# An adaLN condition and a feed-forward layer on one core: how q is projected, and who scales the first batch

## Chip, cores and metric

One core of one Trainium2 chip runs the whole kernel. The metric is the device time of one execution in microseconds, a median over runs. The engines are named TensorE (PE), its weight loads (PEld), VectorE (DVE), ScalarE (ACT), GpSimd (POOL) and SyncE (SP), as in the profile.

## Reference, cut to what matters

`x` is 16 x 512 x 1024, `cond` 16 x 512, all fp32.

```
q_emb = relu(cond @ W3 + b3)                     # 16 x 1024
u     = (512 * x + sum_over_512_rows(x)) * q_emb[:, None, :]
v     = relu(u @ W2 + b2)
ffn   = v @ W_base + b_base + (v @ A_s) @ B_s + routed low-rank experts(v)
out   = x + ffn
```

Everything waits for `q_emb`: no row of `u` exists without it. It is a small product (16 x 512 by 512 x 1024) in full fp32.

## The kernel before, in words

Data lie transposed: features on the 128 partitions, the 512 tokens of a batch in the free dimension. D = 1024 makes K = 8 tiles, or two halves of H = 4. Batches go in NP = 8 pairs (a, b); one pair is `g`, and for each pair the product with W2 is made as NPROD = 7 half-size products n = 0..6 (a Strassen scheme), later the same again with W_base. A product has H operand tiles k and H output tiles j. Each fp32 product is three matmuls in fp32r (function `three`): high x high, low x high, high x low; so both operands are split into a rounded high part (`act_hi`, `w_hi`) and a rest (`act_lo`, `w_lo`). TensorE runs 12 matmuls for each k of the first three products (`first_groups`), in the order k outer, j inner; each k waits for `lo_done` and `w2_lo_done`.

The order on every engine is written out by hand, one block per engine; each engine works its instructions off in order. DMAs are issued by SyncE and, six at the start, by ScalarE. Each 256 KB tile of W3 (`w3_raw`, half h, row block k), of W2 (`r11`, `r12`, ...) and of x (`src`) is one DMA.

The head of the kernel, which the change touches, before:

- TensorE warms up on `zeros` (`warm`), then `project(0, ...)` makes q's first half with the condition (128 x 16) as the held operand and W3's rows (128 x 512) streamed, so q lands as 16 rows by 512 in one bank. A copy to `qrow`, four transposes (`turn`) and q is feature-major, 128 x (4 x 16), in `q_tok`.
- VectorE's `condition(h)` adds b3 and makes relu(q) twice: `qn` (times T = 512) and `q1`.
- For x of batch a (quadrant G11) ScalarE sums each raw tile while q is not there (`first_total`), VectorE scales it by `qn` (`first_scale`) and multiplies the sum by `q1` to get the shift; ScalarE rounds the high part (`first_hi`), VectorE makes the low part (`low`). ScalarE also rounds W2's first tiles (`first_w2`), VectorE makes their low part (`first_w2_low`).
- The second half of W3 is projected before product 0 (`project(1, ...)`), copied by ScalarE, and transposed by `turn(1)` behind product 0's first k.
- `x_scale` is the one-instruction form used for the other quadrants: ScalarE scales a tile by `qn` and sums it in the same instruction.

ScalarE's function table is loaded by an ACT_TABLE_LOAD that the build puts right ahead of ScalarE's first ACTIVATE, behind any wait that stands alone in front of it.

Of the kernel before, what the change touches and what calls it, by code (L numbers as in the profile page):

```python
# [5 lines left out]
F32 = mybir.dt.float32  # L6
# [31 lines left out]
def adaln_ffn(nc, xT, condT, w3, w2, b2, wbase, bbase, acat, bcat, brouter, outT, E, R):  # L38
# [18 lines left out]
    with ExitStack() as ctx:  # L57
# [28 lines left out]
        qrow = sb("qrow", [NB, D], F32, early)  # L86
# [34 lines left out]
        q1 = sb("q1", [P, K, NB], F32, stage1)  # L121
# [4 lines left out]
        ident = sb("ident", [P, P], F32, stage1)  # L126
        sb("pad8", [P, T - K - 2 * K * NB - 9 * H - P], F32, stage1)
# [37 lines left out]
        Q_BANK, QT_BANK, WARM_BANK = 4, 6, 0  # L165
        q_tok = [ps[:, QT_BANK + h, 0:HALF * NB].rearrange("p (m b) -> p m b", b=NB) for h in range(2)]
# [9 lines left out]
        q_copied = sem("q_copied")  # L176
        q_turned = sem("q_turned")
# [18 lines left out]
        first_sum = sem("first_sum")  # L196
        first_mean = sem("first_mean")
        first_x1 = sem("first_x1")
# [84 lines left out]
        def scaled_no(i, q, k):  # L283

            return H * (i - (q == G11)) + k + 1
# [23 lines left out]
        def _(sp):  # L309
# [68 lines left out]
            load_w3(0, 2)  # L378
            load_w3(1, 0)
            load_x(0, G11, 0)  # L380
            load_w3(1, 2)
            for k in range(1, H):
                load_x(0, G11, k)
                load_w2(Q11, r11, k)
            for k in range(H):
                load_x(0, G21, k)
                load_w2(Q12, r12, k)
# [194 lines left out]
        def _(pool):  # L582

            nc.gpsimd.memset(ident[:], 0.0).then_inc(const_step, 1)
# [4 lines left out]
            pool.wait_ge(const_step, 2)  # L589
            nc.gpsimd.affine_select(out=ident[:], in_=ident[:], compare_op=ALU.not_equal, fill=1.0, base=0,  # L590
                                    pattern=[[-1, P]], channel_multiplier=1).then_inc(const_step, 1)
# [3 lines left out]
            def shift_of(i, q, ks=range(H)):  # L595

                for k in ks:
                    if q == G12:
                        pool.wait_ge(t1_made, four(i, k))
                    else:  # L600
                        pool.wait_ge(x_scaled[q], scaled_no(i, q, k))
# [34 lines left out]
        def _(act):  # L636
            def x_scale(i, q, k):
# [3 lines left out]
                if i == 0:  # L641
                    act.wait_ge(q_ready, 1 + HALF_OF[q])
                nc.scalar.activation(src[:, t, :], src[:, t, :], ACT.Identity,  # L643
# [106 lines left out]
            def first_hi(k):  # L750
                act.wait_ge(first_x1, k + 1)
# [4 lines left out]
            def first_w2(k):  # L756
                act.wait_ge(w2_loaded[H * Q11 + k], 16)
                nc.scalar.activation(w_hi[:, 0, k, :], r11[:, k, :], ACT.Copy).then_inc(first_hi_done, 1)

            def first_total(k):  # L760

                t = tile(G11, k)
                act.wait_ge(x_loaded[t], 16)
                nc.scalar.activation(act_lo[:, slot(0, 1, k), :], src[:, t, :], ACT.Copy,
                                     accum_out=vsum[:, t:t + 1]).then_inc(first_sum, 1)
# [3 lines left out]
            act.dma_start(w3_raw[:, 0, 3], w3[0, 3]).then_inc(w3_loaded[3], 16)  # L769
            act.dma_start(w3_raw[:, 1, 1], w3[1, 1]).then_inc(w3_loaded[QK + 1], 16)  # L770
            act.dma_start(r11[:, 0, :], w2[0, 0]).then_inc(w2_loaded[H * Q11], 16)
            act.dma_start(w3_raw[:, 1, 3], w3[1, 3]).then_inc(w3_loaded[QK + 3], 16)

            first_total(0)
            first_w2(0)
            first_hi(0)
            first_total(1)
            first_w2(1)
            act.wait_ge(q_sum, 2)
            nc.scalar.activation(qrow[:, D // 2:D], ps[0:NB, Q_BANK + 1, :], ACT.Copy).then_inc(q_copied, 1)  # L780
            first_total(2)
            first_hi(1)
            first_w2(2)
# [1054 lines left out]
```

## Time and profile before

| | |
|---|---|
| median of 3 runs | 1411.69 us (1411.1 to 1412.03) |
| the profiled execution | 1411.89 us, its span 1410.1 us |
| TensorE busy | 1405.7 us (100%), 6175 matmuls |
| VectorE, ScalarE, GpSimd busy | 910.6, 605.5, 22.1 us |
| PEclk | 9 (of 9) in all 40 slices |

The span runs from the first to the last instruction; 1.8 us of the execution lie outside it. Busy shares are of the span. The chain that ended last is followed back from the last instruction. PEclk is the clock that the throttle granted; it says nothing of a lower level in the first microseconds, which shows in the spacing of matmuls of one size.

### The profile page before, as it was taken

Reading aid. Unit: us, or ns where it says so; the run is one execution under the profiler, and the core shown is the slowest. Engines: PE = TensorE matmul, PEld = TensorE weight load, DVE = VectorE, ACT = ScalarE, POOL = GpSimd, SP = SyncE. Lnnn points to the kernel's source line nnn. Section 1 sums busy time; section 2 is a strip of 40 time slices with the busy share of each in tenths; the row PEclk is TensorE's granted clock in tenths of the full one; section 3 lists DMA queues with packets and bytes.
Section 4 is the critical chain, followed back from the end, with each engine's and each line's share of the span. In section 5 each row is a group of like instructions: output and inputs, shape, how many; then the busy total and the mean of one; then the engine's idle time right before and its main releaser. Section 6 shows DMA issues by size and latency. Waiting matters only on the chain.

```text
span 1410.1 us, 18033 instructions
## 1 busy us (share of the span) xinstructions
PE 1405.7 (100%) x6175; PEld 1155.8 (82%) x6175; DVE 910.6 (65%) x1563; ACT 605.5 (43%) x1136; POOL 22.1 (2%) x69
## 2 busy tenths in 40 slices
PE   9999999999999999999999999999999999999999
PEld 5888888888888888888888888888888888888887
DVE  6987565765656656567889665655655656556564
ACT  6774645546455464645544231332312323132230
POOL 3000000000000000000000000000000000000000
PEclk9999999999999999999999999999999999999999
DMA  8252414334142342426726527163361724617242
GB/s 314 67 173 82 155 54 139 106 90 155 52 141 98 104 148 59 142 83 224 266 89 208 195 95 249 61 222 136 109 239 63 246 105 136 216 60 258 94 148 91
DMA packets 135580, 200.03 MB, mean 142 GB/s; under 512 B 38752, under 2 KB 39008, under 8 KB 135488
## 3 DMA queue, kind: packets, MB, share of 16 engines
q1 hardware_dynamic: 134480, 197.39, 42.4%
q10 hardware_dynamic: 1008, 1.48, 0.3%
q8 instruction: 49, 0.80, 0.2%
q14 instruction: 43, 0.35, 0.1%
HBM read 127.12 MB, written 71.70 MB: 141 GB/s over the span
## 4 chain that ended last, share of the span: by engine, by line
PE 99%; DMA 0%; DVE 0%; DVEq 0%; issue 0%
PE ps L1611 33%; PE ps L1613 33%; PE ps L1612 33%; PE ps L1619 1%; DMA cond_b<-in_condT 0%; PE ps L1628 0%; DVE buf L1604 0%; DVEq L57 0%; PE ps L1634 0%
## 5 line engine op out<-in xcount | busy, mean ns | idle before, releaser
L1611 PE MATMUL ps<-act_hi,w_hi 128*128 128x512 f32 x1792 | 697.4, 389 | 0.0
L1612 PE MATMUL ps<-act_lo,w_hi 128*128 128x512 f32 x1792 | 697.1, 389 | 0.0
L1613 PE MATMUL ps<-act_hi,w_lo 128*128 128x512 f32 x1792 | 697.1, 389 | 0.0
L1611 PEld LDWEIGHTS ps<-act_hi,w_hi 128*128 128x128 f32 x1792 | 336.3, 188 | 70.1 <-DVE act_lo L1078 0.3
L1613 PEld LDWEIGHTS ps<-act_hi,w_lo 128*128 128x128 f32 x1792 | 336.3, 188 | 70.0
L1612 PEld LDWEIGHTS ps<-act_lo,w_hi 128*128 128x128 f32 x1792 | 336.3, 188 | 69.8
L681 ACT ACTIVATE act_hi<-src 128x512 fp32r<-128x512 f32 x256 | 156.4, 625 | 256.1 <-PE ps L1613 254.3
L1142 DVE SCALAR_TENSOR_TENSOR buf<-ps,bb_sb,buf 128x512 f32<-128x512 f32 x127 | 95.0, 749 | 157.3 <-PE ps L1613 142.3
L1085 DVE TENSOR_TENSOR act_lo<-src,act_hi 128x512 fp32r<-128x512 f32 x192 | 130.4, 684 | 36.5 <-ACT act_hi L681 36.5
L1078 DVE SCALAR_TENSOR_TENSOR act_lo<-src,shift,act_hi 128x512 fp32r<-128x512 f32 x128 | 95.2, 748 | 31.2 <-ACT act_hi L678 30.6
L700 ACT ACTIVATE yhi<-buf 128x512 fp32r<-128x512 f32 x128 | 80.0, 625 | 64.2 <-PE ps L1613 64.1
L1142 DVE SCALAR_TENSOR_TENSOR buf<-ps,b_sb,buf 128x512 f32<-128x512 f32 x92 | 68.8, 750 | 51.2 <-PE ps L1613 50.5
L1085 DVE TENSOR_TENSOR act_lo<-buf,act_hi 128x512 fp32r<-128x512 f32 x64 | 43.4, 687 | 84.6 <-ACT act_hi L681 84.5
L678 ACT ACTIVATE act_hi<-src,shift 128x512 fp32r<-128x512 f32 x124 | 87.5, 714 | 14.1 <-POOL shift L603 13.8
L708 ACT ACTIVATE buf<-ps 128x512 f32<-128x512 f32 x64 | 37.9, 597 | 120.5 <-PE ps L1613 120.5
L716 ACT ACTIVATE buf<-ps 128x512 f32<-128x512 f32 x64 | 37.9, 597 | 118.4 <-PE ps L1613 118.4
L1182 DVE TENSOR_TENSOR buf_lo<-buf,yhi 128x512 fp32r<-128x512 f32 x64 | 44.1, 688 | 55.5 <-ACT yhi L700 54.7
L727 ACT ACTIVATE buf<-ps 128x512 f32<-128x512 f32 x60 | 35.9, 598 | 84.1 <-PE ps L1613 84.1
L643 ACT ACTIVATE src<-src,qn 128x512 f32<-128x512 f32 x92 | 65.5, 712 | 0.9 <-DVE q L1047 0.9
L1082 DVE SCALAR_TENSOR_TENSOR act_lo<-src,act_hi 128x512 fp32r<-128x512 f32 x64 | 44.0, 688 | 33.2 <-ACT act_hi L681 33.1
L1611 PE MATMUL ps<-yhi,a_hi 128*128 128x512 f32 x128 | 49.8, 389 | 0.0
L1612 PE MATMUL ps<-buf_lo,a_hi 128*128 128x512 f32 x128 | 49.8, 389 | 0.0
(114 smaller groups left out, 1020.6 us busy)
## 6 DMA issues: line engine op xcount, KB each, us to landing
src<-in_xT SPq DMA_DIRECT2D x224, 256.0 KB, 2.9
y_scratch<-buf SPq DMA_DIRECT2D x128, 256.0 KB, 2.1
src<-y_scratch SPq DMA_DIRECT2D x128, 256.0 KB, 5.0
outT<-buf SPq DMA_DIRECT2D x127, 256.0 KB, 3.9
buf<-in_xT SPq DMA_DIRECT2D x32, 256.0 KB, 4.8
wl_raw<-in_wbase SPq DMA_DIRECT2D x6, 1024.0 KB, 5.9
r<-in_w SPq DMA_DIRECT2D x15, 256.0 KB, 9.6
grow<-gates_scratch SPq DMA_DIRECT2D x96, 32.0 KB, 2.1
```

Source lines behind the costliest of these rows:

```text
L643: nc.scalar.activation(src[:, t, :], src[:, t, :], ACT.Identity, scale=qn[:, H * HALF_OF[q] + k, 2 * i + BATCH_OF[q]:2 * i + BATCH_OF[q] + 1],
L678: nc.scalar.activation(act_hi[:, slot(g, n, k), :], source[:, t, :], ACT.Identity, bias=shift[:, t:t + 1]).then_inc(hi_done, 1)
L681: nc.scalar.activation(act_hi[:, slot(g, n, k), :], source[:, t, :], func).then_inc(hi_done, 1)
L700: nc.scalar.activation(yhi[:, (y_no(i, c, j) - 1) % 2, :], buf[:, j, :], func).then_inc(yhi_done, 1)
L1078: nc.vector.scalar_tensor_tensor(act_lo[:, s, :], source, shift[:, t:t + 1], act_hi[:, s, :].bitcast(F32), ALU.add, ALU.subtract).then_inc ...
L1082: nc.vector.scalar_tensor_tensor(act_lo[:, s, :], source, 0.0, act_hi[:, s, :].bitcast(F32), ALU.max, ALU.subtract).then_inc(lo_done, 1)
L1085: nc.vector.tensor_tensor(act_lo[:, s, :], source, act_hi[:, s, :].bitcast(F32), ALU.subtract).then_inc(lo_done, 1)
L1142: nc.vector.scalar_tensor_tensor(buf, ps[:, bank, :], bias, buf, ALU.add, ALU.add).then_inc(done, 1)
L1182: nc.vector.tensor_tensor(lo, y, hi, ALU.subtract).then_inc(ylo_done, 1)
L1611: nc.tensor.matmul(out, wh, a_h, start=start, stop=False, skip_group_check=onto)
L1612: nc.tensor.matmul(out, wh, a_l, start=False, stop=False, skip_group_check=onto)
L1613: return nc.tensor.matmul(out, wl, a_h, start=False, stop=stop, skip_group_check=onto)
```

## The change

It does these things:

1. `project` swaps the operands: each 128 x 128 block of W3 is held, the condition (128 x 16) is streamed. q comes out feature-major, with no copy and no transpose: 4 matmuls for each k, 32 in all in place of 8 matmuls and 8 transposes. `qrow`, `q1`, `ident`, `turn` go.
2. Batch a's first tiles are scaled and summed by ScalarE's `x_scale`, which waits for q; VectorE only multiplies the sum by 1/T (`first_shift`). `first_total` and `first_scale` go.
3. Of W3's second half, k = 0 is projected before product 0, k = 1 behind its first k, k = 2 and 3 behind its second. `condition(1)` stands behind product 0's last `low`.
4. 7 warm-up matmuls ahead and 6 between the halves, for 6 and 1.
5. The first tiles of x and W2 are loaded in two halves of 64 partitions, one by each queue; W3's second half is loaded later. ScalarE has seven DMA issues in front where it had six.

```diff
+            sp.dma_start(src[0:P // 2, tile(G11, 0), :], xT[0, 0, 0:P // 2]).then_inc(x_loaded[tile(G11, 0)], 16)
+            sp.dma_start(r11[0:P // 2, 0, :], w2[0, 0, 0:P // 2]).then_inc(w2_loaded[H * Q11], 16)
             load_w3(1, 0)
-            load_x(0, G11, 0)
+            load_w2(Q11, r11, 1)
+            load_x(0, G11, 2)
             load_w3(1, 2)
+            load_w3(1, 3)
...
                 if i == 0:
                     act.wait_ge(q_ready, 1 + HALF_OF[q])
+                    if t == tile(G11, 0):
+                        act.wait_ge(first_x_rest, 16)
...
+            act.dma_start(src[P // 2:P, tile(G11, 0), :], xT[0, 0, P // 2:P]).then_inc(first_x_rest, 16)
+            act.dma_start(r11[P // 2:P, 0, :], w2[0, 0, P // 2:P]).then_inc(first_w2_rest, 16)
+            act.dma_start(src[:, tile(G11, 1), :], xT[0, 1]).then_inc(x_loaded[tile(G11, 1)], 16)
             act.dma_start(w3_raw[:, 1, 1], w3[1, 1]).then_inc(w3_loaded[QK + 1], 16)
...
+            for k in range(H):
+                x_scale(0, G11, k)
+                first_w2(k)
+                first_hi(k)
             x_scale(0, G21, 0)
-            first_hi(3)
...
-                dve.wait_ge(q_turned, h + 1)
-                nc.vector.tensor_tensor(part, q_tok[h], bias, ALU.add).then_inc(q_biased, 1)
+                dve.wait_ge(q_sum, h + 1)
+                nc.vector.tensor_tensor(part, q_banks[h], bias, ALU.add).then_inc(q_biased, 1)
+                dve.wait_ge(q_biased, h + 1)
+                nc.vector.tensor_scalar(part, part, 0.0, float(T), ALU.max, ALU.mult).then_inc(q_ready, 1)
...
+            def first_shift(k):
                 t = tile(G11, k)
+                dve.wait_ge(x_scaled[G11], scaled_no(0, k))
+                nc.vector.tensor_scalar(shift[:, t:t + 1], vsum[:, t:t + 1], 1.0 / T, None,
                                         ALU.mult).then_inc(first_mean, 1)
+            for k in range(H):
+                first_shift(k)
                 first_w2_low(k)
                 low(0, 0, k)
+            condition(1)
...
-                    mm = nc.tensor.matmul(ps[0:NB, Q_BANK + h, :], cond_sb[:, k, :], w3_raw[:, h, k, :],
-                                          start=(k == 0), stop=(k == QK - 1))
+                    for m in range(HALF):
+                        mm = nc.tensor.matmul(ps[:, h * HALF + m, 0:NB],
+                                              w3_raw[:, h, k, m * P:(m + 1) * P], cond_sb[:, k, :],
+                                              start=(k == 0), stop=(k == QK - 1))
...
             pe.wait_ge(warm_set, 1)
-            warm(6)
+            warm(7)
             pe.wait_ge(cond_loaded, 16)
             project(0, range(QK))
+            warm(6)
             project(1, (0,))
-            pe.wait_ge(const_step, 3)
-            turn(0)
-            project(1, range(1, QK))
-            warm(1)
...
-                    if k == 0 and n == 0:
-                        turn(1)
+                    if n == 0 and k < 2:
+                        project(1, ((1,), (2, 3))[k])
```

**TensorE, from the first instruction to product 0.** A row is one matmul of the program, or xN equal ones; an fp32 one is executed as two weight loads and two passes. L1634 warms, L1619 projects, L1628 transposes, L1611 to L1613 are product 0. Before:

```order
L1634 MATMUL ps<-zeros 128x512 x6
L1619 MATMUL ps<-w_raw,cond_b 16x512 x5
L1628 MATMUL ps<-ident,qrow 128x16 x4
L1619 MATMUL ps<-w_raw,cond_b 16x512 x3
L1634 MATMUL ps<-zeros 128x512
L1611 MATMUL ps<-act_hi,w_hi 128x512
L1612 MATMUL ps<-act_lo,w_hi 128x512
L1613 MATMUL ps<-act_hi,w_lo 128x512
```

With the change (L1600 warms, L1592 projects, L1582 to L1584 are product 0):

```order
L1600 MATMUL ps<-zeros 128x512 x7
L1592 MATMUL ps<-cond_b,w_raw 128x16 x16
L1600 MATMUL ps<-zeros 128x512 x6
L1592 MATMUL ps<-cond_b,w_raw 128x16 x4
L1582 MATMUL ps<-act_hi,w_hi 128x512
L1583 MATMUL ps<-act_lo,w_hi 128x512
L1584 MATMUL ps<-act_hi,w_lo 128x512
```

The first projection is 16 small matmuls in place of 4 long ones, the transposes are gone, six warm-ups stand behind it, and one quarter of the second half's projection is left ahead of product 0.

**TensorE, behind the twelve matmuls of a k of product 0.** Before, behind k = 0:

```order
L1612 MATMUL ps<-act_lo,w_hi 128x512
L1613 MATMUL ps<-act_hi,w_lo 128x512
L1628 MATMUL ps<-ident,qrow 128x16 x4
L1611 MATMUL ps<-act_hi,w_hi 128x512
L1612 MATMUL ps<-act_lo,w_hi 128x512
```

With the change, behind k = 1 (behind k = 0 stand four):

```order
L1583 MATMUL ps<-act_lo,w_hi 128x512
L1584 MATMUL ps<-act_hi,w_lo 128x512
L1592 MATMUL ps<-cond_b,w_raw 128x16 x8
L1582 MATMUL ps<-act_hi,w_hi 128x512
L1583 MATMUL ps<-act_lo,w_hi 128x512
```

Eight projecting matmuls stand between the second and the third k, and four between the first and the second, where four transposes stood behind the first.

**ScalarE, from its last DMA issues to the second tile** (with the semaphores that each row, or a wait that stands alone ahead of it, waits for). Before:

```order
L772 DMA w_raw<-in_w 128x512
L764 ACT_TABLE_LOAD
L764 ACTIVATE act_lo,vsum<-src 128x512 [waits x_loaded0]
L758 ACTIVATE w_hi<-r 128x512 [waits w2_loaded0]
L753 ACTIVATE act_hi<-src,shift 128x512 [waits first_mean,first_x1]
L764 ACTIVATE act_lo,vsum<-src 128x512 [waits x_loaded1]
L758 ACTIVATE w_hi<-r 128x512 [waits w2_loaded1]
L780 ACTIVATE qrow<-ps 16x512 [waits q_sum]
L764 ACTIVATE act_lo,vsum<-src 128x512 [waits x_loaded2]
```

With the change (L644 is `x_scale`):

```order
L766 DMA r<-in_w 64x512
L767 DMA src<-in_xT 128x512
L768 DMA w_raw<-in_w 128x512
L644 ACT_TABLE_LOAD [waits first_x_rest,q_ready]
L644 ACTIVATE src,vsum<-src,qn 128x512 [waits x_loaded0]
L760 ACTIVATE w_hi<-r 128x512 [waits first_w2_rest,w2_loaded0]
L753 ACTIVATE act_hi<-src,shift 128x512 [waits first_mean]
L644 ACTIVATE src,vsum<-src,qn 128x512 [waits q_ready,x_loaded1]
L760 ACTIVATE w_hi<-r 128x512 [waits w2_loaded1]
```

The table load stands behind the waits for q (`q_ready`) and for the second half of x's first tile, where it stood behind no wait; the sum of the raw tile is gone, and the first thing that ScalarE computes needs q.

## Rows read from the trace of the kernel before

**Rows 1.** The page: chain that ended last, by line.
```profile
PE ps L1611 33%; PE ps L1613 33%; PE ps L1612 33%; PE ps L1619 1%; DMA cond_b<-in_condT 0%; PE ps L1628 0%; DVE buf L1604 0%; DVEq L57 0%; PE ps L1634 0%
```

**Rows 2.** Timeline, TensorE: start us, us, engine, line, op, tiles, count.
```profile
1.17 2.74 PE L1634 MATMUL ps<-zeros 128*128 128x512 bf16 x6 [1.17 <-DVE zeros L1240]
...
4.02 5.98 PE L1619 MATMUL ps<-w_raw,cond_b 128*16 128x512 f32 x10
...
13.37 0.50 PE L1611 MATMUL ps<-act_hi,w_hi 128*128 128x512 f32 x1
```

**Rows 3.** Timeline, TensorE's weight loads of the first projection.
```profile
5.39 0.10 PEld L1619 LDWEIGHTS ps<-w_raw,cond_b 128*16 128x16 f32 x1 [1.25 <-DMA w_raw<-in_w]
...
5.70 0.15 PEld L1619 LDWEIGHTS ps<-w_raw,cond_b 128*16 128x16 f32 x1 [0.21 <-issue]
...
6.55 0.15 PEld L1619 LDWEIGHTS ps<-w_raw,cond_b 128*16 128x16 f32 x1 [0.70 <-issue]
...
7.72 0.09 PEld L1619 LDWEIGHTS ps<-w_raw,cond_b 128*16 128x16 f32 x1 [0.37 <-DMA w_raw<-in_w]
```

**Rows 4.** Timeline, from the projection to product 0's first operand.
```profile
3.68 1.28 ACT L764 ACT_TABLE_LOAD   x1 [3.68 <-issue]
...
8.83 0.63 ACT L764 ACTIVATE act_lo<-src 128x512 fp32r<-128x512 f32 x1 [3.87 <-DMA src<-in_xT]
...
9.18 0.68 DVE L1242 COPY qrow<-ps 16x512 f32<-16x512 f32 x1 [8.06 <-PE ps L1619]
...
10.00 0.39 PE L1628 MATMUL ps<-ident,qrow 16*128 16x16 f32 x4
...
10.50 0.22 DVE L1044 TENSOR_TENSOR q<-ps,cond_b 128x64 f32<-128x64 f32 x1 [0.65 <-PE ps L1628]
10.52 0.63 ACT L758 ACTIVATE w_hi<-r 128x512 fp32r<-128x512 f32 x1 [0.97 <-DMA r<-in_w]
...
10.76 0.20 DVE L1046 TENSOR_SCALAR qn<-q 128x64 f32<-128x64 f32 x1
...
12.56 0.75 DVE L1078 SCALAR_TENSOR_TENSOR act_lo<-src,shift,act_hi 128x512 fp32r<-128x512 f32 x1 [0.25 <-ACT act_hi L753]
```

**Rows 5.** Timeline, a scale with its sum on ScalarE.
```profile
18.21 0.18 DVE L1047 TENSOR_SCALAR q<-q 128x64 f32<-128x64 f32 x1
...
18.48 0.72 ACT L643 ACTIVATE src<-src,qn 128x512 f32<-128x512 f32 x1 [0.86 <-DVE q L1047]
...
19.21 0.71 ACT L753 ACTIVATE act_hi<-src,shift 128x512 fp32r<-128x512 f32 x1
```

**Rows 6.** Timeline, weight loads of full blocks and of transposes.
```profile
9.97 0.32 PEld L1628 LDWEIGHTS ps<-ident,qrow 16*128 16x128 f32 x4 [0.90 <-issue]
...
13.36 0.19 PEld L1611 LDWEIGHTS ps<-act_hi,w_hi 128*128 128x128 f32 x1 [0.27 <-DVE act_lo L1078]
...
13.47 0.19 PEld L1612 LDWEIGHTS ps<-act_lo,w_hi 128*128 128x128 f32 x1
```

**Rows 7.** Timeline, TensorE around the second set of transposes.
```profile
16.01 0.39 PE L1613 MATMUL ps<-act_hi,w_lo 128*128 128x512 f32 x1
...
16.33 0.42 PE L1628 MATMUL ps<-ident,qrow 16*128 16x16 f32 x4
...
16.67 0.50 PE L1611 MATMUL ps<-act_hi,w_hi 128*128 128x512 f32 x1
...
17.01 0.40 PE L1612 MATMUL ps<-act_lo,w_hi 128*128 128x512 f32 x1
```

**Rows 8.** Timeline, products 0 and 2: operands against their matmuls.
```profile
19.57 0.39 PE L1611 MATMUL ps<-act_hi,w_hi 128*128 128x512 f32 x1
...
22.60 0.75 DVE L1078 SCALAR_TENSOR_TENSOR act_lo<-src,shift,act_hi 128x512 fp32r<-128x512 f32 x1 [0.28 <-ACT act_hi L678]
...
39.83 0.68 DVE L1085 TENSOR_TENSOR act_lo<-buf,act_hi 128x512 fp32r<-128x512 f32 x1
...
41.33 0.39 PE L1611 MATMUL ps<-act_hi,w_hi 128*128 128x512 f32 x1
```

## What the change should do to the time, predicted before it ran

> **What bounds the kernel now.** I read the chain of waits first: TensorE's three matmul lines hold 33% of the span each, so the end is TensorE's [rows 1]. The page's table says the same, 1405.7 us busy of 1410.1. The reader is to see that nothing counts but what delays TensorE's first product matmul and what is put between its product matmuls; VectorE's 65% and ScalarE's 43% don't. So I went to the timeline of the first 25 us. Product 0 starts at 13.37 us [rows 2]. From then on the spacing of product matmuls is 0.227 us: the third k of product 0 starts at 19.57 and the third k of product 2 at 41.33, 96 matmuls apart [rows 8]. The one thing between them is the second set of transposes.
>
> In the head, the last tile of W3's first half lands just before 7.72, where its weight load stops waiting for it [rows 3]. VectorE's copy of q can start at 9.18; transposes, bias, scale, shift, high and low part follow, and the low part starts at 12.56, takes 0.75 and releases TensorE [rows 4]. That chain is what the change reorders.
>
> The clock of TensorE: the six warm-ups of 512 columns begin (2.74 - 0.63)/5 = 0.42 us apart, the last one's record being 0.63 long [rows 2], which is 1.2 GHz. A projecting pass takes 0.85 at that level (loads at 5.70 and 6.55 [rows 3]) and half of that at 2.4. Ten passes start from 4.02 and end at 10.00, the last one starting about 9.4 [rows 2]; nine steps in 5.39 us are 3.6 of 0.853 and 5.4 of 0.427. So the rise to 2.4 GHz came near 7.1 us, 5.9 us after TensorE's first matmul at 1.17, with TensorE streaming 512 columns nearly without a break until then.
>
> **The change, part by part.**
>
> *Projecting matmuls.* An fp32 matmul is two weight loads, each with its pass, so a k of one half is 4 x 2 = 8 loads of 128 x 128 and 8 passes of 16 columns. The trace has no such pair. The load sets its price, since 16 columns are little. Nearest row for it: at product 0's start the second load of a 128 x 128 fp32r block begins 0.11 us after the first [rows 6]. From below: transposes load 16 x 128, four in 0.32 us, 0.08 each [rows 6]. From above: both rows are of the high clock; if loads go at half speed at 1.2 GHz, 0.22. I take 0.11, the same shape.
> The Trainium skill (TensorE: Matmul & The Clock Gate, LDWEIGHTS) says that a weight load costs its columns over 1.2, whatever its rows: 107 ns for both shapes. The 0.11 agrees; the transposes' 0.08 does not. By the rule the 24 pairs below cost 2.6 us, by the transposes' row 1.9.
>
> *When q is there.* At 0.11, k = 0 takes 4.02 to 4.9 and later ones wait for their tiles (5.39, at most 6.55, 7.72 [rows 3]). The DMAs ahead of that last tile are unchanged in bytes: where the other queue's third transfer was a tile of W3, there are now two half tiles. So the last k is done at 7.72 + 8 x 0.11 = 8.6, plus 0.2 for the last pass's way out: 8.8, against 9.1.
>
> *From q to product 0.* Bias 0.1 later (transposes end at 10.39, bias starts 10.50): 8.9. Scale starts 0.26 after the bias and takes 0.20 [rows 4]: 9.36. ScalarE reacts 0.09 after VectorE's end (18.39 to 18.48 [rows 5]): 9.45. Now the table load: 1.28 us. Before, it ran at 3.68 while ScalarE waited for data [rows 4]; now it stands behind the wait for q, so nothing hides it: 10.73. The scale with its sum holds ScalarE 0.73 (18.48 to 19.21 [rows 5]): 11.46. W2's high part, queued ahead of x's, 0.63 [rows 4]: 12.09; beside it the accumulator's read and VectorE's shift, a column each, fit. High part 0.71 [rows 5]: 12.80. Low part 0.75 and two hand-overs of 0.05: 13.65. The second half tiles of x and W2 (W2's first tile landed by 10.52 before [rows 4]) are needed at 10.73 and 11.46 and hidden. So product 0 starts at about 13.65 for 13.37: **+0.3**. Without the table load it would be 1.0 earlier than now. The warm-ups (six at 0.43 from 8.6: to 11.2) and one k (to 12.1) end before it.
>
> *Between product matmuls.* 12 projecting matmuls, 24 pairs x 0.11 = 2.6, and two re-entries of 0.11 (the second matmul after a break starts 0.34 after the first, 16.67 to 17.01, not 0.23 [rows 7]): 2.9. The transposes go: 16.01 to 16.67 less 0.23, and one re-entry, 0.55 [rows 7]. **+2.3.** The matmuls of this piece are all on TensorE's own path, nothing covers them.
>
> *The clock.* Before, product 0 begins at 2.4 GHz. Now TensorE streams for 3.0 us (seven warm-ups), then only 16 columns at a time for 4.4 us with waits, six warm-ups (2.6 us), loads again, then a wait for product 0. Whether that brings the rise before product 0, no row shows. If not, product 0 starts at 1.2 GHz; if then it takes the 5.9 us of matmuls that it took from 1.17, a product matmul costs 0.427 for 0.227 in that time, and 5.9 x (1 - 0.227/0.427) = 2.8 is lost. Bounds: 0 and 2.8. In what preceded the rise of before, TensorE streamed nearly all the time; that is the row this stretch is unlike, so I take **+2.8**.
>
> *Hidden parts.* VectorE loses four scales, a copy and one relu, off the path. `condition(1)` now comes behind the second k's projection, just ahead of product 0's third k. From there: bias and scale 0.5, first scale and sum of quadrant G21 0.8, GpSimd's shift 0.7, high part 0.7, hand-overs 0.2: its low part starts 3.0 after the third k begins. Before, it started 22.60 - 19.57 = 3.03 after it [rows 8]. So products 1 and 2 see VectorE's queue where they saw it, relative to TensorE; the tightest place, product 2's third k, has its low part at 39.83 + 0.68 = 40.51 and starts at 41.33 [rows 8], 0.8 spare. If that is used up, the excess is paid once: below 1 us.
>
> *Sum.* 0.3 + 2.3 + 2.8 = 5.4. The profiled execution took 1411.89, 0.20 over the median of the runs, so 1411.7 + 5.4 = **1417.0 us**.
>
> **Rivals.**
>
> A. *The clock stays or comes up* (the small matmuls count as work, or the warm-ups suffice). No loss of 2.8: 1411.7 + 2.6 = 1414.3. For it: TensorE is never without instructions for long; against: its streaming share falls to an eighth or so (16 of some 130 columns' time).
>
> B. *Weight loads take 0.22 at the low clock.* Then TensorE, not the DMAs, bounds the projection: 32 loads x 0.22 = 7.0 from 4.1, q at 11.3 instead of 8.8. +2.5: 1419.5. It decides from 0.12 us a load on, where 8 loads no longer fit between two tiles.
>
> C. *The table load brings more than its row.* Behind it ScalarE's first scale would start later than 10.73. In the trace of before ScalarE idles 3.87 us behind the load, waiting for x [rows 4], and that much may hide there: the price lies between 0 and 3.9. I take a second length of the row, 1.3: 1418.3.
> The Trainium skill (ScalarE: Activation LUTs, What ACT_TABLE_LOAD costs) has a drain of about 1380 ns behind the load's 1283; the row's 1.28 agrees with the load, no row here shows the drain, and by the page this rival's time would be 1418.4.
>
> D. *Not slower.* Loads at 0.08 or less as the transposes' [rows 6], clock up before product 0. Start: 0.25 less, +0.05; between: 24 x 0.08 + 0.2 - 0.55 = 1.6. 1413.4, within what can be told from no change; with loads at half of that again, 1412.2. It decides below about 0.11 a load, and only if A holds.
>
> E. *Faster.* It takes product 0's start before 10.5 us, and q can't be there before 8.3 with 3.5 us of chain behind it, the table load left out. Nearly excluded.
>
> **How the numbers follow.** Forecast (low clock into product 0, loads 0.11) 0.37; B 0.20; C 0.10; A 0.19; D 0.12; E and the unforeseen 0.02. 0.2% of this time, 2.8 us, is about what a measurement can tell from no change: 1408.9 to 1414.5. Slower: forecast, B, C and some of A, 0.68; same: D and most of A, 0.30; faster 0.02. Range: from D's lower form to B with a little of the second k's projection at the low clock as well (8 x 0.11 = 0.9): 1412.8 to 1420.2.
>
> **What would show it.** The weight loads' spacing in the 32 projecting pairs (0.11, or 0.22); q's bias on VectorE at 8.9; the table load at 9.4, behind q's scale; product 0's first matmul at 13.65; its matmuls 0.427 apart at first and 0.227 after; TensorE's gap for 4 and for 8 projecting matmuls 0.9 and 1.8 us. The forecast is wrong if product 0 begins at 0.227, or if q comes after 9.5.

## The result, and the profile after

| | before | changed |
|---|---|---|
| median, us | 1411.68 (1411.1 to 1412.03, 6 executions) | 1417.09 (1413.95 to 1418.27, 6 executions) |
| ratio | | 1.0036 [1.0024, 1.0049] |
| profiled execution, its span | 1411.89, 1410.1 | 1416.22, 1414.4 |

The changed kernel is slower by 0.36%, and the forecast of 1417.0 is met to 0.1 us. That closeness is partly luck. The six executions were 1413.95, 1416.07, 1416.22, 1417.95, 1418.05 and 1418.27: the median falls between two groups where no execution lies. The kernel before shows nothing of the kind; its six lie within 1 us. The ratio is over the 0.2% that can be told from no change, so the side, slower, was right as well, and the range held.

The page after, chain that ended last, by engine and by line (answers to [rows 1]):

```profile
PE 99%; DMA 0%; DVE 0%; issue 0%; ACT 0%; ACTq 0%; DVEq 0%
PE ps L1582 33%; PE ps L1583 33%; PE ps L1584 33%; PE ps L1592 0%; DMA w_raw<-in_w 0%; ACT src L644 0%; DVE w_lo L1034 0%; DVE act_lo L1061 0%; ACT w_hi L760 0%; DVE buf L1575 0%; ACTq L762 0%; DVEq L57 0%; DVE qn L1028 0%; DVE qn L1030 0%; ACT L644 0%
```

The end is still TensorE's, but the table load's line, L644, and ScalarE's W2 rounding now stand in the chain: the way from q to product 0 runs through ScalarE. The timeline of the head shows it (answers to [rows 2, 4]):

```profile
1.17 3.17 PE L1600 MATMUL ps<-zeros 128*128 128x512 bf16 x7 [1.17 <-DVE zeros L1222]
...
4.13 1.06 PE L1592 MATMUL ps<-cond_b,w_raw 128*128 128x16 f32 x8
...
5.54 3.33 PE L1592 MATMUL ps<-cond_b,w_raw 128*128 128x16 f32 x24 [0.35 <-DMA w_raw<-in_w]
...
8.98 0.23 DVE L1028 TENSOR_TENSOR qn<-ps,cond_b 128x64 f32<-128x64 f32 x1 [7.87 <-PE ps L1592]
...
9.24 0.20 DVE L1030 TENSOR_SCALAR qn<-qn 128x64 f32<-128x64 f32 x1
9.51 1.28 ACT L644 ACT_TABLE_LOAD   x1 [9.51 <-DVE qn L1030]
...
10.80 0.72 ACT L644 ACTIVATE src<-src,qn 128x512 f32<-128x512 f32 x1
...
12.78 0.75 DVE L1061 SCALAR_TENSOR_TENSOR act_lo<-src,shift,act_hi 128x512 fp32r<-128x512 f32 x1
...
13.59 0.79 PE L1582 MATMUL ps<-act_hi,w_hi 128*128 128x512 f32 x1 [0.64 <-DVE act_lo L1061]
...
18.24 0.40 PE L1584 MATMUL ps<-act_hi,w_lo 128*128 128x512 f32 x1
...
18.47 0.96 PE L1592 MATMUL ps<-cond_b,w_raw 128*128 128x16 f32 x8
...
19.28 0.47 PE L1582 MATMUL ps<-act_hi,w_hi 128*128 128x512 f32 x1
...
21.90 0.39 PE L1584 MATMUL ps<-act_hi,w_lo 128*128 128x512 f32 x1
...
22.13 1.85 PE L1592 MATMUL ps<-cond_b,w_raw 128*128 128x16 f32 x16
...
23.83 0.49 PE L1582 MATMUL ps<-act_hi,w_hi 128*128 128x512 f32 x1
```

The row of 8 at 4.13 holds one k's four matmuls, two passes each, and 8 passes in 1.06 us, of which the last record alone is 0.26, are 0.11 apart. From q's bias at 8.98 one reads down the chain: table load, scale, low part, product 0 at 13.59. The twelve matmuls of product 0's first k take 18.47 - 13.59 = 4.88 us, where they took 16.01 + 0.23 - 13.37 = 2.87 before [rows 2, 7]. The windows say why (us, then its length, busy time of PE, PEld, DVE, ACT and POOL with the number of instructions, PEclk, DMA share, GB/s):

```profile
4.00:7.70 3.70, 3.35 (x29) 3.19 (x28) 0.00 (x0) 0.00 (x0) 0.00 (x0) 1.00 1.03 295
7.70:13.50 5.80, 5.25 (x21) 3.67 (x20) 1.90 (x6) 3.98 (x8) 0.00 (x0) 0.50 1.05 378
13.50:17.90 4.40, 4.31 (x10) 3.44 (x11) 3.30 (x9) 4.40 (x10) 1.12 (x1) 0.50 1.05 387
17.90:24.00 6.10, 6.10 (x40) 5.42 (x40) 1.50 (x2) 0.36 (x1) 2.19 (x3) 0.99 1.05 387
```

The granted clock was 2.4 GHz while q was projected, fell to 1.2 GHz at 7.7 us, in the middle of the 16-column matmuls, and was back at 18.0. The rise had come by 4.4 us, as the projection began (0.11 a pass from there on), and the fall came in the projection's last quarter.

This execution is 1414.4 - 1410.1 = 4.3 us longer in its span. Three terms add up to it:

| | predicted | measured |
|---|---|---|
| start of product 0 | 13.65, +0.3 | 13.59, +0.2 |
| projecting matmuls between product matmuls | +2.3 | (0.81 + 0.08) + (1.70 + 0.10) - 0.55 = +2.1 |
| lower clock into product 0 | +2.8 | 4.88 - 2.87 = +2.0 |
| sum, of unrounded terms | +5.4 | +4.4 |

(0.81 is 19.28 less the 18.47 at which the next product matmul would have started, 1.70 likewise; 0.08 and 0.10 are re-entries.)

### The profile page after: what moved, and what is told of

It is laid out like the page before. It is cut to its first block, busy times and chain, and to the rows that moved or that the text cites. A ratio compares the mean times of both kernels' runs of the same rounds, so it can differ in the third digit from the quotient of the medians.

```text
span 1414.4 us, 18116 instructions
## 1 busy us (share of the span) xinstructions
PE 1409.2 (100%) x6221; PEld 1165.5 (82%) x6221; DVE 907.6 (64%) x1556; ACT 605.3 (43%) x1135; POOL 21.1 (1%) x67
## 4 chain that ended last, share of the span: by engine, by line
PE 99%; DMA 0%; DVE 0%; issue 0%; ACT 0%; ACTq 0%; DVEq 0%
PE ps L1582 33%; PE ps L1583 33%; PE ps L1584 33%; PE ps L1592 0%; DMA w_raw<-in_w 0%; ACT src L644 0%; DVE w_lo L1034 0%; DVE act_lo L1061 0%; ACT w_hi L760 0%; DVE buf L1575 0%; ACTq L762 0%; DVEq L57 0%; DVE qn L1028 0%; DVE qn L1030 0%; ACT L644 0%
## 5 line engine op out<-in xcount | busy, mean ns | idle before, releaser
L1582 PE MATMUL ps<-act_hi,w_hi 128*128 128x512 f32 x1792 | 698.4, 390 | 0.6 <-DVE act_lo L1061 0.6
L1584 PE MATMUL ps<-act_hi,w_lo 128*128 128x512 f32 x1792 | 697.8, 389 | 0.0
L1582 PEld LDWEIGHTS ps<-act_hi,w_hi 128*128 128x128 f32 x1792 | 337.0, 188 | 70.6 <-DVE act_lo L1061 0.7
L1584 PEld LDWEIGHTS ps<-act_hi,w_lo 128*128 128x128 f32 x1792 | 336.9, 188 | 70.1
L644 ACT ACTIVATE src<-src,qn 128x512 f32<-128x512 f32 x96 | 68.3, 712 | 6.3 <-DVE qn L1030 6.3
L1582 PE MATMUL ps<-yhi,a_hi 128*128 128x512 f32 x128 | 49.8, 389 | 0.0
```

What stands on the lines that cost most here:

```text
L1582: nc.tensor.matmul(out, wh, a_h, start=start, stop=False, skip_group_check=onto)
L1584: return nc.tensor.matmul(out, wl, a_h, start=False, stop=stop, skip_group_check=onto)
```

## The experiments

All times are medians with the range and the number of executions. The kernel before, run beside them, had 1411.51 (22 executions), 1411.46 (29) and 1411.33 (9) in the three groups in which they ran.

**The changed kernel again.** No edit.

> The changed kernel once more, for more executions: its times so far fall into 1414 (clock risen at 4 us and high at product 0), 1416 (risen at 4 us, fallen in the projection) and 1418 us (low until product 0). Theory (the change costs 0.2 by the start, 2.1 between the products and 0, 2.0 or some 4.3 us by the clock): no execution under 1413.5 or over 1419, about a third at 1418, a spread of 4 us beside 1 us of the kernel before. Rival (the three groups were chance or a disturbed chip): one group, within 1 us.

Measured: 1418.01 (1416.28 to 1418.28, 5), ratio 1.0042 [1.0028, 1.0055]. The groups held, with three of these five in the slowest where a third was expected. With the first six there are eleven executions: one at 1413.95, four from 1416.07 to 1416.38, six from 1417.95 to 1418.28. The mean granted clock sorts them: 0.999 for the first, 0.996 to 0.998 for the four, 1.000 for the six. In the profile above TensorE is at half clock for 18.0 - 7.7 = 10.3 us, which is 0.36% of the span: 0.996. The profile taken here was one of the six, 1418.15 with a span of 1416.3. Its timeline:

```profile
4.13 6.85 PE L1592 MATMUL ps<-cond_b,w_raw 128*128 128x16 f32 x32
...
11.09 0.22 DVE L1028 TENSOR_TENSOR qn<-ps,cond_b 128x64 f32<-128x64 f32 x1 [9.98 <-PE ps L1592]
...
11.62 1.28 ACT L644 ACT_TABLE_LOAD   x1 [11.62 <-DVE qn L1030]
...
15.70 0.80 PE L1582 MATMUL ps<-act_hi,w_hi 128*128 128x512 f32 x1 [0.64 <-DVE act_lo L1061]
...
19.28 0.54 PE L1584 MATMUL ps<-act_hi,w_lo 128*128 128x512 f32 x1
...
19.65 0.39 PE L1582 MATMUL ps<-act_hi,w_hi 128*128 128x512 f32 x1
...
20.34 0.96 PE L1592 MATMUL ps<-cond_b,w_raw 128*128 128x16 f32 x8
```

The 32 loads take 6.85 us, 0.213 each, in one row without a wait for a tile: the weight loads of a TensorE at 1.2 GHz bound the projection, q's bias comes at 11.09 in place of 8.98 and product 0 at 15.70. Product 0's matmuls go 0.43 apart until 19.28. PEclk reads 1.00 over this whole stretch, as it does ahead of the first rise in the kernel before; a level that was never left doesn't show there and is read from the spacing. The first k of product 0 takes 20.34 - 15.70 = 4.64 us (its last matmul starts at 20.12, 0.23 before the next one could). Sum: start +2.3, between +2.1, clock 4.64 - 2.87 = +1.8, together 6.2; the spans differ by 6.2. This is rival B's mechanism. By their times the slowest group is of this kind, 6 of 11, the commonest of the three cases; one of the six was profiled.

**Table load early.** A one-column ACTIVATE ahead of ScalarE's wait for q takes the load with it.

```diff
...
+            act.wait_ge(warm_set, 1)
+            nc.scalar.activation(touch[:], zeros[:, 0:1], ACT.Copy)
             for k in range(H):
                 x_scale(0, G11, k)
```

> The changed kernel, with a one-column ACTIVATE of ScalarE on the zeros tile ahead of its waits, so that the table load is done by 6 us. Theory (the table load behind q_ready costs 1.28 us of the path): q's bias stays at 9.0 us, ScalarE's first scale starts at 9.5 in place of 10.8, and x's first low part is ready at 12.3. TensorE's small matmuls end only at 12.6 at the low clock and 11 at the high one, so product 0 starts at 12.3 to 12.8 for 13.59, and the kernel takes 0.8 to 1.3 us less than the changed one. Rival (something else on ScalarE, such as a drain or the half tiles' landing, holds the first scale): the scale starts at 10.8 as before and the time stays.

Measured: 1415.18 (1412.38 to 1417.74, 11), ratio 1.0028 [1.0019, 1.0037]; four executions at 1417.43 to 1417.74, three at 1412.38 to 1412.91, four between. Its profile (1412.91, span 1411.1), timeline:

```profile
4.48 1.28 ACT L772 ACT_TABLE_LOAD   x1 [4.48 <-issue]
...
8.52 0.22 DVE L1031 TENSOR_TENSOR qn<-ps,cond_b 128x64 f32<-128x64 f32 x1 [7.41 <-PE ps L1595]
...
9.06 0.72 ACT L645 ACTIVATE src<-src,qn 128x512 f32<-128x512 f32 x1 [3.09 <-DVE qn L1033]
...
11.85 0.50 PE L1585 MATMUL ps<-act_hi,w_hi 128*128 128x512 f32 x1
12.18 0.39 PE L1586 MATMUL ps<-act_lo,w_hi 128*128 128x512 f32 x1
```

The scale starts 0.54 behind q's bias; with the load in between it was 10.80 - 8.98 = 1.82, so the load cost its 1.28 and nothing else. The granted clock fell here too, but was back before product 0 began (windows):

```profile
7.70:11.00 3.30, 3.30 (x12) 1.83 (x12) 1.15 (x4) 1.94 (x5) 0.00 (x0) 0.50 1.05 387
```

Product 0 starts 1.5 earlier than in the kernel before, the matmuls between cost the same 2.1: +0.6, where the spans differ by +1.0. The other 0.4 lies far behind the head, at the first matmul that reads `buf_lo` (timeline):

```profile
76.80 0.69 DVE L1167 TENSOR_TENSOR buf_lo<-buf,yhi 128x512 fp32r<-128x512 f32 x1 [2.15 <-DMA y_scratch<-buf]
...
77.61 0.19 PEld L1585 LDWEIGHTS ps<-yhi,a_hi 128*128 128x128 f32 x1 [0.53 <-issue]
```

VectorE waits 2.15 us for a DMA and ends at 77.49, and TensorE, whose last matmul started at 77.12, goes on at 77.64 in place of 77.35. In the profile of the streaming run below this place has no gap, though product 0 starts within 0.15 us of here; so the time belongs to when that DMA landed, not to the change. In the slowest group the gain over the changed kernel is only 0.5 (1417.6 for 1418.1). None of it was profiled here, but in the changed kernel's own slow profile TensorE is busy with small matmuls until 15.06 and waits only 0.64 us for the operand, so no more than that is to be had.

**Most of the second half's projection left out.** Of its 16 matmuls 7 remain (all four of k = 0, one of each later k), so q's second half is incomplete and the output too.

```diff
-                    for m in range(HALF):
+                    for m in range(HALF if h == 0 or k == 0 else 1):
...
```

> The changed kernel with 9 of the 12 projecting matmuls between product 0's matmuls left out (the first block column alone is projected for k = 1 to 3 of the second half; q's second half is then incomplete). Theory (each projecting matmul is two weight loads of 0.112 us on TensorE's own path): 18 loads fewer, 2.0 us less than the changed kernel, the start of product 0 unchanged at 13.6. Rival (weight loads of the block matmuls hide under product matmuls, and the time between products goes into waits for operands): under 0.5 us less.

Measured: 1414.27 (1411.59 to 1416.28, 11), ratio 1.002 [1.0011, 1.0029]. Again three groups, 1411.6 to 1411.9, 1413.2 to 1414.4 and 1415.85 to 1416.28, each about 2 us under the changed kernel's. The two gaps between product matmuls went from 1.04 and 1.93 us to 0.36 and 0.59 (timeline):

```profile
16.18 0.29 PE L1592 MATMUL ps<-cond_b,w_raw 128*128 128x16 f32 x2
...
19.14 0.51 PE L1592 MATMUL ps<-cond_b,w_raw 128*128 128x16 f32 x4
```

18 passes fewer bring 2.0 us, 0.11 each: the term of the sum is a real one, and every pass pays. The spread of 4.7 us stays, so it doesn't come from these matmuls. The profile (1411.91, mean clock 0.999) is of the fastest group; the clock fell and was back before product 0 at 13.32 (windows):

```profile
8.30:11.60 3.30, 3.30 (x12) 1.83 (x11) 0.57 (x3) 2.34 (x4) 0.00 (x0) 0.50 1.05 384
```

The execution at 1413.22 has a mean clock of 0.946 without being longer than its neighbours; so the mean sorts the executions well but not without exception, and why it is low there is not known.

**Nine warm-ups for six** behind the projection.

```diff
-            warm(6)
+            warm(9)
             project(1, (0,))
```

> The changed kernel with 9 warm-ups between the halves for 6. Theory (the low clock in product 0 comes from the 16-column matmuls of the projection, and three more warm-ups make the time streamed between the two projections 3.8 us for 2.6): the clock may rise before or soon after product 0's start, at 13.6 to 14.4; product 0's matmuls 0.23 apart earlier than 17.9 us; 0 to 1.5 us less than the changed kernel. Rival (the clock falls because of the wait for product 0's operand, not because of the projection): product 0 still starts low, and the kernel is the same or up to 1.3 us slower since the warm-ups push the start.

Measured: 1416.24 (1413.66 to 1418.55, 6), ratio 1.0031 [1.0019, 1.0042]: two at 1413.7, three at 1416.1 to 1417.1, one at 1418.55. The profile was of the last. Its timeline:

```profile
10.82 4.00 PE L1600 MATMUL ps<-zeros 128*128 128x512 bf16 x9
...
16.18 0.77 PE L1582 MATMUL ps<-act_hi,w_hi 128*128 128x512 f32 x1
```

Nine streamed matmuls at the low level did not bring the clock up before product 0 (0.43 apart until 19.74), and they pushed the second half's k = 0 and product 0 itself from 15.70 to 16.18. Six executions with two of them in the best group are too few to say whether the extra three help the clock in others. Inconclusive by time; no cure either way.

**VectorE's scale back,** the rest of the change kept: ScalarE sums raw tiles ahead of q, VectorE scales by q.

```diff
-            for k in range(H):
-                x_scale(0, G11, k)
-                first_w2(k)
-                first_hi(k)
+            first_total(0)
+            first_w2(0)
+            first_hi(0)
...
```

> The changed kernel with batch a's first tiles summed raw by ScalarE and scaled by VectorE as before; projection, loads and warm-ups as changed. Theory (of the two parts of the change the projection brings q 0.2 us earlier at most, and the scale on ScalarE with its table load makes the chain from q to product 0 longer by 1.2): product 0's first operand is ready by about 12.0 to 12.4 and TensorE itself, busy with its small matmuls until 12.6 at the low clock, becomes the later one; the kernel takes 0.8 to 1.3 us less than the changed one and is still 3 us over the one before. Rival (the scale on ScalarE is as good, and the difference is all clock and interleaved matmuls): the same time as the changed kernel.

Measured: 1416.35 (1414.99 to 1417.78, 5), ratio 1.0033 [1.0021, 1.0046]. Its profile (1414.99, span 1413.2) has the same low-clock head as the repeat of the changed kernel, with q's bias at the same 11.09 (timeline):

```profile
11.09 0.22 DVE L1049 TENSOR_TENSOR q<-ps,cond_b 128x64 f32<-128x64 f32 x1 [9.98 <-PE ps L1626]
...
13.26 0.75 DVE L1083 SCALAR_TENSOR_TENSOR act_lo<-src,shift,act_hi 128x512 fp32r<-128x512 f32 x1 [0.25 <-ACT act_hi L765]
...
13.33 1.15 PE L1626 MATMUL ps<-cond_b,w_raw 128*128 128x16 f32 x8
14.33 0.47 PE L1616 MATMUL ps<-act_hi,w_hi 128*128 128x512 f32 x1
14.65 0.39 PE L1617 MATMUL ps<-act_lo,w_hi 128*128 128x512 f32 x1
```

From q's bias to product 0 it is 3.24 for 4.61 us: ScalarE's scale, table load and all, costs 1.37 on this way. Not all that the operand gained shows in it: the low part ends at 14.01, and TensorE's projecting matmuls hold product 0 until 14.33, as the expectation had it. Up to the start of the low part it is 13.26 - 11.09 = 2.17 us, where the repeat of the changed kernel has 14.89 - 11.09 = 3.80: ScalarE's scale costs 1.6 there, and 1.28 of it is the table load. The clock was up by then. Sum +1.0, +2.1 and nothing for the clock: +3.1, as the spans say. By their times alone five executions, spread over 2.8 us, don't tell the gain.

**Streaming between the projecting matmuls.** The early table load, and one 512-column warm-up behind every second projecting matmul of the first half; eight for six behind it.

```diff
...
+                        if h == 0 and m % 2 == 1 and (k, m) != (QK - 1, HALF - 1):
+                            warm(1)
...
-            warm(6)
+            warm(8)
```

> The table load early (as in e1), and one 512-column warm-up after each pair of projecting matmuls of the first half (seven in all), 8 warm-ups behind it for 6. Theory (a clock that has risen falls because TensorE streams only 16 columns at a time in the projection): with the warm-ups between them the clock does not fall again, and where it was low at the start it rises during the projection; q comes 1.2 to 2.6 us later than in e1's profile, product 0 starts at 13.1 to 14.4 at 0.23 us a matmul in every execution, the times lie within 1.5 us of each other (e1: 5.4), median 1413.4 to 1414.7. Rival (chance places the clock's rise and fall whatever TensorE streams): a spread of 4 us or more, and the median above e1's 1415.2 by the later q.

Measured: 1413.09 (1412.63 to 1419.62, 12), ratio 1.0024 [1.0012, 1.0036]. Eight executions lie at 1412.63 to 1413.38, one at 1417.38 and three at 1419.5 to 1419.6; all twelve have a mean clock of 1.000. The windows of its profile (1412.63):

```profile
4.00:8.00 4.00, 4.00 (x36) 3.83 (x35) 0.00 (x0) 1.49 (x2) 0.00 (x0) 1.00 1.05 313
8.00:12.00 4.00, 3.09 (x22) 2.11 (x21) 2.01 (x6) 2.80 (x7) 0.00 (x0) 1.00 1.06 388
```

The fall at 7.7 is gone, and in none of twelve executions does the mean show one, where it did in six of the eleven with the early table load alone; the group at 1413.9 to 1415.9 vanishes. So the string of 16-column matmuls loses the clock and streaming between them keeps it. That TensorE's short waits for W3's tiles (0.35 us in the changed kernel's profile) did it is the less likely reading: in the last run below TensorE has no wait from 4.1 us on and the clock falls near 12. The rest of the expectation failed: product 0 starts at 11.98 in the profile, not at 13.1 to 14.4, four of the twelve lie outside 1.5 us, and the spread is 7.0, as the rival had it; the median is below the expected 1413.4. What stays is the other case, argued and not profiled: where the rise has not come when the projection begins, every added warm-up costs 0.43 us for 0.21, and three of these executions are slower than any of the changed kernel.

**The scale alone.** The kernel before with ScalarE's scale, its table load behind the wait for q; projection, transposes and loads as before.

```diff
-            first_total(0)
+            x_scale(0, G11, 0)
             first_w2(0)
             first_hi(0)
-            first_total(1)
+            x_scale(0, G11, 1)
             first_w2(1)
...
```

> The kernel before with one part of the change alone: batch a's tiles scaled and summed by ScalarE, the table load behind the wait for q; projection, transposes, loads and warm-ups as before. Theory: from q at 11.06 the table load 1.28, the scale 0.73, W2's high part 0.53, the high part 0.71 and the low part 0.75 put product 0 at 15.2 for 13.37; 1.9 us over the kernel before, with the narrow spread of before, since TensorE streams 512 columns as before (it then waits 2.3 us, which could let the clock fall: up to 2 us more). Rival (the scale on ScalarE is free): the time of before.

Measured: 1414.29 (1412.69 to 1414.7, 11), ratio 1.0015 [1.0006, 1.0024]; five executions at 1412.69 to 1413.32 with a clock of 1.000, six at 1414.29 to 1414.7 with 0.998 or 0.999. The five lie 1.7 over the kernel before, where 1.9 was expected, so the scale is not free. Timeline and windows of one of the six:

```profile
10.45 1.28 ACT L643 ACT_TABLE_LOAD   x1 [10.45 <-DVE q L1044]
...
11.74 0.72 ACT L643 ACTIVATE src<-src,qn 128x512 f32<-128x512 f32 x1
...
14.53 0.50 PE L1598 MATMUL ps<-act_hi,w_hi 128*128 128x512 f32 x1 [1.73 <-DVE act_lo L1075]
```

```profile
11.90:15.30 3.40, 1.67 (x6) 0.77 (x5) 1.98 (x5) 3.40 (x8) 0.00 (x0) 1.00 1.05 387
15.30:18.80 3.50, 3.50 (x10) 2.68 (x8) 1.86 (x4) 3.50 (x9) 1.97 (x3) 0.51 1.05 386
```

TensorE waited 1.73 us for the operand, and shortly after product 0 had begun the granted clock fell to 1.2 GHz for 3.4 us; eight matmuls began 0.43 in place of 0.23 apart, 1.6 in all. Here 512 columns were streamed all through the projection and the few transposes are those of the kernel before, whose executions show no fall, so small matmuls can't be its cause; the long wait is what is new here. It doesn't bring a fall each time: by the program the five other executions wait too.

**The scale alone, table load early.** As above with the one-column ACTIVATE ahead.

```diff
+            act.wait_ge(warm_set, 1)
+            nc.scalar.activation(touch[:], zeros[:, 0:1], ACT.Copy)
             x_scale(0, G11, 0)
```

> As e6, with the one-column ACTIVATE ahead so that the table load is done by 6 us. Theory: 1.28 us less than e6, product 0 at 13.95, 0.6 us over the kernel before. Rival (the table load brings a drain of its own behind it, so that hiding it brings more than its row): 2.6 us less than e6.

Measured: 1411.67 (1411.26 to 1412.92, 11), ratio 1.0002 [0.9993, 1.001]: no difference from the kernel before, and all eleven at a clock of 1.000. Timeline:

```profile
3.61 1.28 ACT L775 ACT_TABLE_LOAD   x1 [3.61 <-issue]
...
11.10 0.72 ACT L644 ACTIVATE src<-src,qn 128x512 f32<-128x512 f32 x1 [5.99 <-DVE q L1047]
...
13.88 0.50 PE L1601 MATMUL ps<-act_hi,w_hi 128*128 128x512 f32 x1 [0.22 <-DVE act_lo L1078]
```

Against the five undisturbed executions of the run above (median 1413.12) it gains 1.45 us, near the table load's 1.28. The other six of that run (median 1414.6) paid 1.5 more, for the clock. That the fall comes from the wait is argued from these two runs: with 0.22 us of wait left there is none. Waits of 0.91 and 1.06 us just ahead of product 0, in the profiles of the streaming run and of the run with half the projection left out, brought none either. The expected 0.6 over the kernel before is 0.2 in the medians.

**A version meant to fit.** Blocks held, but the loads and the scale of before; two warm-ups behind each k of the first half, and of the second half three k projected before product 0 and one behind its first k.

```diff
...
-            warm(6)
-            project(1, (0,))
+            project(1, (0, 1, 2))
...
+                    if k < QK - 1:
+                        if h == 1 and k == 0:
+                            pe.wait_ge(q_ready, 1)
+                        warm(2, 0 if h == 1 else WARM_BANK)
...
-                    if n == 0 and k < 2:
-                        project(1, ((1,), (2, 3))[k])
+                    if n == 0 and k == 0:
+                        project(1, (3,))
```

> A version put together from the parts that pay: q by held blocks, raw sums and VectorE's scale as before, loads in the order of before, three quarters of the second half projected by blocks ahead of product 0 with two warm-ups behind each k, the last quarter behind product 0's first k. Theory: where the clock is high from the projection on, q's bias at 9.5 to 10, product 0 at 12.5 to 13.2, 0.5 us between product matmuls; 0.5 us under to 0.3 over the kernel before. Where it is low up to 7 us, q comes 1.5 later and the kernel is 1 to 1.5 us slower than before. Rival (the warm-ups don't hold the clock): like the changed kernel, 2 to 5 us slower, with a wide spread.

Measured: 1415.31 (1414.48 to 1420.01, 5), ratio 1.0034 [1.0022, 1.0046]. Its profile (1414.77) has product 0 at 13.48, hardly later than before, but the granted clock was lost again (windows):

```profile
8.00:12.00 4.00, 4.00 (x35) 3.60 (x32) 2.25 (x7) 2.68 (x7) 0.00 (x0) 0.98 1.05 401
12.00:13.40 1.40, 1.40 (x7) 1.13 (x8) 1.40 (x5) 1.40 (x4) 0.00 (x0) 0.50 1.05 386
13.40:18.50 5.10, 5.10 (x13) 3.98 (x12) 4.91 (x9) 3.22 (x7) 2.18 (x3) 0.50 1.05 386
```

It fell near 12 us, behind a stretch with many more small matmuls than warm-ups. The streaming run had as many passes to a warm-up in its projection and kept the clock; how the warm-ups must lie is not shown. The rival came true: 3.9 us slower, with a spread of 5.5. No kernel tried here beats the kernel before; the scale alone with the early table load equals it.

## Why the prediction was right, and where it was lucky

*When q is there.* Predicted 8.9, measured 8.98, with the loads at the 0.11 taken from [rows 6]. True where the clock rises as the projection begins, as it did in the profiled execution and, by their times, not in six of eleven. The prediction named a q later than 9.5 as a sign that it is wrong; in the profile of the slowest group q's bias came at 11.09, so by its own sign the forecast fails there. Its other sign, a product 0 that begins at 0.227, was seen in neither profile of the changed kernel.

*From q to product 0.* Predicted 13.65, measured 13.59. The table load lay on the path behind the wait for q as worked out, at 9.51 for 9.4. Its place is shown by both early-load runs. This and the term before hold for the first profile; in the other product 0 starts at 15.70.

*Between product matmuls.* 2.3 predicted, 2.1 measured: 24 passes at 0.112, with re-entries of 0.08 and 0.10. The run that leaves nine projecting matmuls out gives back 2.0.

*The clock.* The sum took 2.8, for a product 0 that starts at 1.2 GHz and a rise 5.9 us later. Measured 2.0 in one profile and 1.8 in the other: the first k of product 0 was slow in both, but only that k, since the rise came 4.4 and 3.9 us after product 0's start. The term had the level at product 0's start right and was too large by 0.8 to 1.0. What the step didn't see is that the clock could be up already during the projection and be lost there. It had only the one rise of the kernel before, near 7.1, to go by; here it came by 4.4, from where on the loads are 0.11 apart.

*Rival B, set at 0.20, was the commonest case.* The step that failed is the pricing of the loads apart from the clock. The forecast assumed both that the clock is still at 1.2 GHz when product 0 begins and that the projection runs at the upper level's 0.11. Without the rise and fall in between, which it didn't think of, the two don't go together. A sum that keeps the clock low throughout has rival B's start, measured at +2.3, with less left for product 0 to lose (+1.8 for +2.8): 6.2 in all, 1417.9, against the 1418.0 to 1418.3 of those executions. B's own 1419.5 added both in full. So 1417.0 lies 0.8 over the middle group, which is the case it describes, because its clock term was too large, and the median landed beside it because the six executions split evenly between two groups; of all eleven the median is 1417.95.

*Slips in the prediction's own arithmetic.* B's onset, 0.12 us a load, doesn't follow from its rows: 16 loads fit between 5.39 and 7.72 up to 0.146. The measured 0.213 is past both. And the range's ends, 1412.8 and 1420.2, aren't those of the terms it names, 1412.2 and 1419.5 + 0.9 = 1420.4. The measured 1417.09 lies well inside either.

*Rival A* (no clock loss, 1414.3) is perhaps the single execution at 1413.95. It was not profiled; its mean clock of 0.999 is what the early-load run and the variant without most of the second half had in profiles where the clock fell and was back before product 0. So the clock was probably not kept there, as A has it, but lost and regained in time.

*Rival C* is out. The ACTIVATE behind the load starts at 10.80, 0.01 after 9.51 + 1.28. The Trainium skill (ScalarE: Activation LUTs, What ACT_TABLE_LOAD costs) adds to the load a drain of about 1380 ns for every switch to a different set; no trace here shows it at this first load, and the early-load runs price the load at 1.3 to 1.45.

*Rival D* would have needed loads under 0.11 with the clock up; they were never quicker than 0.112. *Rival E* would have needed a product 0 before 10.5, and the earliest in any profile here is 11.85. The Trainium skill (TensorE: Matmul & The Clock Gate, LDWEIGHTS) puts a load of 128 columns at 107 ns: the 0.112 at 2.4 GHz agrees, the 0.213 at 1.2 GHz doesn't.

*Hidden parts.* The page's group of the first matmul of each k, with TensorE's idle time ahead of it in the whole execution:

```profile
L1582 PE MATMUL ps<-act_hi,w_hi 128*128 128x512 f32 x1792 | 698.4, 390 | 0.6 <-DVE act_lo L1061 0.6
```

The 0.6 us is the wait at 13.59. Products 1 and 2 never wait, so moving `condition(1)` cost nothing, as predicted.

Open are why the first rise comes at such different times from one execution to the next, and why the spread of times is absent in the kernel before. The rise itself varies there as well: in the three profiles whose TensorE head is that of before, the projecting passes of 512 columns are 0.43 apart from 7.26, 5.37 and 4.83 us on. But q's bias stays between 9.81 and 10.50, since in two of them TensorE is ahead of W3's last tile and waits for it (0.16 and 0.90 us).

## What to carry to other kernels

A matmul with few columns is priced by its weight loads, and those follow TensorE's clock: swapping the operands so that the small matrix is streamed saves copy and transposes, but it put 2.1 us on TensorE's path here and made the start depend on whether the clock was up. Price everything on TensorE at both levels and add up only sums that are consistent in the clock; if the profile of one execution can't tell which holds, look at the spread over several. And look where the first ACTIVATE stands: behind a wait its table load is on the path, and one dummy ACTIVATE ahead of the wait takes it off.

## What the runs showed of the hardware

- The first rise to 2.4 GHz came by 4.4 us in one profiled execution of the changed kernel and at 19.3 to 19.7 us in the other, with the same instructions from the start; with VectorE's scale back it came between 13.3 and 14.3, in the eight projecting passes ahead of product 0.
- Loads of 128 x 128 fp32 blocks followed each other at 0.112 us at 2.4 GHz and 0.213 at 1.2 GHz.
- The granted clock fell while 16-column matmuls ran (at 7.7 us, from 2.4 to 1.2 GHz), and in the variant with the scale alone at 15.3, shortly behind a wait of 1.73 us; with 512-column matmuls put between the small ones it didn't fall in twelve executions.
- Behind the kernel's first table load the next ACTIVATE starts 0.01 us later (9.51 + 1.28 to 10.80, and 10.45 + 1.28 to 11.74).
